# Gated cross-attention with a mixture of experts: TensorE's wait for its own last mix product is taken out

## The reference

```python
xn = layernorm(layernorm(x), gamma, beta)
q = (xn @ w_q).reshape(B, SQ, 16, 64)
k, v = split(context @ w_kv)
attn = softmax(einsum('bqhd,bkhd->bhqk', q * 64 ** -0.5, k))
out = einsum('bhqk,bkhd->bqhd', attn, v).reshape(B, SQ, 1024) @ w_out + b_out
x = x + tanh(g_xattn) * tanh(gate) * out
...
logits = layernorm(x) @ gate_w.T + gate_b
weights, selected = top_k(softmax(logits), 2)       # experts 8 and 9 are null
x = x + tanh(g_ffn) * sum over the chosen e of weight_e * (layernorm(x) @ expert_w[e] + expert_b[e])
```

## Time and profile before

| | |
|---|---|
| median of 3 runs | 1507.19 us (1505.58 to 1510.52) |
| span of the profiled execution, first to last instruction | 1490.5 us |
| TensorE busy | 1322.5 us, 7181 products |
| VectorE busy | 1148.4 us |
| ScalarE busy | 795.4 us |
| GpSimd busy | 707.9 us |

### The profile page before, as it was taken

The page is one execution under the profiler, slowest core; times in us unless marked ns, Lnnn a source line. Parts: engine busy times, 40 slices in busy tenths (PEclk is TensorE's granted clock), DMA queues, the critical chain, the costliest instruction groups (busy, mean ns, idle before and its releaser), DMA issues. The chain is left out here.

```text
span 1490.5 us, 31236 instructions
## 1 busy us (share of the span) xinstructions
PE 1322.5 (89%) x7181; PEld 677.1 (45%) x7182; DVE 1148.4 (77%) x2891; ACT 795.4 (53%) x2843; POOL 707.9 (47%) x651
## 2 busy tenths in 40 slices
PE   5576699999999999999999999998069998899997
PEld 3422254444444444444444444543035554455543
DVE  5877688889888888889889888986447775567765
ACT  5765566656555655665566556663244442344442
POOL 0360123244544444454454454354457774666675
PEclk9896899999999999999999999999579999999999
DMA  5895588799887788987787977766344443677773
GB/s 192 223 249 171 159 171 194 185 210 216 214 203 171 177 208 197 239 192 172 179 218 197 239 171 178 178 162 146 136 127 159 156 151 100 219 250 232 243 237 113
DMA packets 415499, 280.70 MB, mean 188 GB/s; under 512 B 319965, under 2 KB 348701, under 8 KB 415054
## 3 DMA queue, kind: packets, MB, share of 16 engines
q1 hardware_dynamic: 387598, 205.85, 56.3%
q0 software_dynamic: 27840, 74.18, 15.8%
HBM read 123.62 MB, written 83.07 MB: 139 GB/s over the span
## 5 line engine op out<-in xcount | busy, mean ns | idle before, releaser
L952 ACT ACTIVATE expd<-scores,less 128x77 f32<-128x77 f32 x1024 | 317.3, 328 | 229.9 <-DVE less L1048 228.8
L851 PE MATMUL scores<-m_sb,zT 128*128 (+2 forms) x2304 | 416.3, 339 | 21.8 <-PEq L156 9.6
L866 PE MATMUL mix<-u_sb,pT 128*128 128x512 f16 x1728 | 383.5, 380 | 0.5 <-DVE x_out L1073 0.4
L1792 PE MATMUL out_bank<-w_parts,m_sb 128*128 x1440 | 336.1, 384 | 1.2 <-issue 0.4
L851 PEld LDWEIGHTS scores<-m_sb,zT 128*128 128x128 f16 x2304 | 223.6, 98 | 190.9 <-issue 30.5
L866 PEld LDWEIGHTS mix<-u_sb,pT 128*128 128x128 f16 x1728 | 168.8, 98 | 197.8 <-DVE x_out L1073 0.7
L952 ACT ACTIVATION_READ_ACCUMULATOR expd<-scores,less 128x1 f32 x1024 | 213.4, 208 | 0.0
L1792 PEld LDWEIGHTS out_bank<-w_parts,m_sb 128*128 128x128 f16 x1440 | 142.2, 99 | 151.2 <-issue 12.0
L1485 POOL DMA_INDIRECT table<-payload,row_i x128 | 159.2, 1244 | 54.3 <-issue 33.5
L1399 POOL TENSOR_TENSOR z_parts<-z,z_parts 128x512 f16<-128x512 f32 x62 | 71.7, 1156 | 208.3 <-ACT z_parts L943 208.3
L1815 ACT CAST m_sb<-yT_bank 128x512 f16<-128x512 f32 x120 | 70.2, 585 | 173.3 <-PE yT_bank L1779 173.3
(11 more groups left out here) (171 smaller groups left out, 1756.5 us busy)
## 6 DMA issues: line engine op xcount, KB each, us to landing
comb<-x_out SPq DMA_DIRECT2D x64, 512.0 KB, 3.2
x_ln<-in_x_dram SPq DMA_DIRECT2D x64, 256.0 KB, 2.7
x_res<-in_x_dram SPq DMA_DIRECT2D x64, 256.0 KB
w_raw<-in_L_ffn_expert_w_dram SPq DMA_DIRECT2D x64, 128.0 KB, 2.3
m_dram<-m_stage SPq DMA_DIRECT2D x32, 231.0 KB, 5.4
u_dram<-m_sb SPq DMA_DIRECT2D x48, 154.0 KB
m_sb<-m_dram SPq DMA_DIRECT2D x12, 616.0 KB
u_sb<-u_dram SPq DMA_DIRECT2D x6, 1024.0 KB, 5.4
```

Of the source, the lines that this page charges most:

```text
L851: last = pe.matmul(scores[s][k][:, 0:n], zT[:, s, zp, t, :], m, start=(t == 0 and (zp, mp) == PRODUCTS[0]), stop=(t == DT - 1 and (zp, mp) ...
L866: last = pe.matmul(mix[:], pT[:, s, pp, k, :], u_sb[:, k, up, :], start=(k == 0 and (pp, up) == PRODUCTS[0]), stop=False)
L952: last = act.activation(expd[:, s, h * KEYS:(h + 1) * KEYS], scores[s][k][:, at:at + KEYS], ACT.Exp, bias=less[:, s, h:h + 1], scale=1.0 / ...
L1792: last = pe.matmul(c.out_bank[s][:], yT[:, s, yp, t, :], w_parts[:, bass.ds(e, 1), t, wp, :].rearrange("p a n -> p (a n)"), start=(t == 0 ...
```

## The change

TensorE's wait and the release behind it are taken out, with the semaphore `mix_ready`. The two that waited for `mix_ready` now wait for `u_read`: the residual of tile i for its count 3i + 3, the turning of p of tile i for 3(i - 1), which is the last mix product of tile i-2. The wait points at the same product as before, without the way over TensorE's sequencer.

```diff
@@ semaphores @@
-        mix_ready = sem("mix_ready")
@@ turn_p_hi(i, s), SyncE @@
                 if later(i, 2):
 
-                    sp.wait_ge(mix_ready, i - 1)
+                    sp.wait_ge(u_read, 3 * (i - 1))
                     sp.nop(nofuse=True)
                 sp.dma_start_transpose(out=pT[:, s, 0], in_=p_parts[:, 0]).then_inc(pT_hi_in[s], 16)
@@ mix_values(i, s), TensorE @@
                 last.then_inc(u_read, 1)
-                pe.wait_ge(u_read, 3 * i + 3)
-                pe.nop(nofuse=True).then_inc(mix_ready, 1)
@@ residual(i, s), VectorE @@
-                dve.wait_ge(mix_ready, i + 1)
+                dve.wait_ge(u_read, 3 * i + 3)
                 dve.wait_ge(x_res_in[s], 8 * (i - s) + 16)
```

## The result

| | before | after |
|---|---|---|
| median of 4 runs | 1508.86 us (1505.58 to 1511.04) | 1464.6 us (1459.26 to 1475.45) |
| ratio, 95% interval | | 0.9708 [0.9675, 0.9741] |
| time of the profiled execution, its span | not given, 1490.5 us | 1463.94 us, 1462.2 us |

The change saves 44.3 us, 2.9%. The forecast was 1470 us with a range of 1465 to 1485, so the time came out 0.4 us under the range. The sign and the place came as forecast, and so did what TensorE gains. The gain was 7 us larger than the sum, because the limit that VectorE was to set was reckoned too early.

A forecast was written before the change was run, and what follows sets the result against it. TensorE was taken to pace attention, losing 3.3 us per loop iteration, with the gain capped by VectorE: 38.6 - 1.5 = 37 us off the 1490.5 us span gives 1453.5, plus 16.7 around it, 1470 us; range 1465 to 1485.

The forecast's parts named there:

- the sum: Attention stage: VectorE's idle time on TensorE, 30.3 + 3.4 + 4.9 = 38.6 us, less 1.5 for small costs: 37 us gained.
- the limit that VectorE was to set: Attention loop: VectorE alone would need 51.8 us per iteration, above TensorE's 51.05, so the gain ends there.
- TensorE paces the stage before: Attention stage: TensorE is never held by anyone and sets the pace, with VectorE close behind.
- Two losses: TensorE between mix and gate: drain, 0.31 us a written-out step, plus register work; 3.3 us per loop iteration go in all.
- only the drain goes: Rival, 15%: between mix and scores, register work and jump stay visible behind the gate; gain 24.6 us, time 1482.5 us.
- 2.04 us before the residual and 0.23 before the scores' maximum: VectorE's idle time on TensorE per loop iteration; with 0.24 for overlap, 2.51 us off 54.35.
- VectorE is late next and takes over the pace: Attention loop after the change: VectorE's 51.8 us per iteration, above TensorE's 51.05, sets the pace; case given 72%.
- the room of some 5.6 us: Attention: with one mix bank TensorE may get some 5.6 us ahead, more than VectorE's steps are uneven.
- mix <- x_out: Sign on TensorE's wait list: this wait for VectorE's reading of the mix appears, with several us.
- The small terms: VectorE's extra register instructions 0.5 us, later u loads at the three batch changes 1 us; 1.5 us subtracted.
- The 16.7 us around the span: Outside the profiled span: 1507.2 - 1490.5 us, if the profiled execution was like the median, and it stays.
- the prediction's first rival: Drain alone goes, 15%, 1482.5 us; by the skill's 166 ns per product 64 x 0.166 = 10.6 us, 1496.6.

The follow-up runs named there:

- experiment 6: A 320-column VectorE multiply added per step: on the kernel before 1490.96 us, ratio 1.0004; on the kernel after 1461.23 us, ratio 0.9803.
- experiment 5: Kernel before plus a second TensorE wait for its own product, behind the first group of u's rows inside the mix: 1509.07 us, ratio 1.0114.
- Experiment 4: Kernel after plus a TensorE wait at the old place, for an older product, five before the mix's last: 1446.59 us, ratio 0.9713.
- experiment 3: Kernel after plus the wait for the last mix product, put behind the gate's eight products: 1479.86 us, ratio 0.9932 to before.
- Experiment 2: Kernel after with TensorE's wait for its last mix product put back, without the release; readers still wait for u_read: 1486.87 us, ratio 0.9985.
- Experiment 8: Kernel after without the mix's last product: 1443.46 us, ratio 0.9704; also with less_top's multiply by a number, one input: 1443.84 us, ratio 0.9700.
- experiment 1: Both kernels rerun unchanged on one chip: before 1488.78 us, ratio 0.9997; after 1447.45 us, ratio 0.9704.
- experiment 7: Kernel after with less_top's multiply by a number, one input: 1444.25 us, ratio 0.9703; also with an extra 320-column VectorE multiply per step: 1457.95 us, ratio 0.9799.

## Why the prediction was right and where it failed

**TensorE paces the stage before: right.** 0.32 us more per step on VectorE cost nothing there (experiment 6), 0.31 us more on TensorE cost 19 us (experiment 5).

**Two losses, the drain (the 0.31 us until TensorE's last product counts as written) and the register work behind it, and both go: right.** The gate begins 0.22 us and the scores 0.42 us after the last product, in the loop and at the jump as forecast. Experiment 4 shows that the same sequencer work is free with a wait that is met early, experiment 3 that it costs 0.28 us, and 0.77 with the jump, behind a wait that isn't. The estimate of 51.05 us for TensorE's iteration measured 51.08. The rival "only the drain goes" is refuted. The Trainium skill, "Advanced Engine Details and Errata", section "Engine Queue Depths", gives TensorE's queue 64 entries; by that the sequencer can be past gate and jump, and the full gain agrees with it.

**Only the readers' half could have done it: no.** Experiment 2 gave some 2 us.

**The step that failed** is "In one iteration it sat 0.95 + 0.45 + 0.64 = 2.04 us before the residual and 0.23 before the scores' maximum", the term from which VectorE's own 51.8 us an iteration and the sum of 38.6 came. It took the list of waits for the whole of VectorE's waiting, and the list leaves out short ones. Two rows of before that I had not set side by side, TensorE's first score bank and VectorE's first maximum:

```profile
618.01 2.51 PE L851 MATMUL scores<-m_sb,zT 128*128 x12 [0.23 <-issue]
```

```profile
634.15 0.64 DVE L1046 TENSOR_REDUCE top<-scores 128x6 f32<-128x462 f32 x1
```

A bank of 12 products takes 2.51 us; the scores of the step at 631.60 have theirs at 634.11, and the maximum begins at 634.15, 0.04 behind it: it waited, and has no bracket. The same 0.04 stands at 593.59 and 607.14 (banks at 593.55 and 607.10), and only the last of these has a bracket, 0.23.

From x_out to the first maximum the four steps took 3.30, 3.27, 3.07 and 3.17 us before, and take 3.14, 2.95, 2.95 and 2.95 after (575.91 - 572.77 and so on): 0.82 us less an iteration where I had 0.23 (the 0.12 of the third step has another cause, which stays open: no bank was awaited there). The rest of each step, from the first maximum to the next x_out, became 1.03, 0.03, 0.53 and 0.72 us shorter: the waits of 0.95, 0.45 and 0.64 with 0.08 each, as reckoned. So the one term that was mis-sized is the 0.23, which is 0.82, 0.70 of it in steps where the maximum waited for its bank.

With it VectorE's own iteration is 54.35 - 2.51 - 0.59 = 51.25 us, measured 51.21. Over the loop that is 12 x 0.59 = 7.1 us more than the 38.6 of the sum, 45.7. Experiment 8 bears it out: with 14 us less for TensorE to do the stage is 832.4 - 786.2 = 46.2 us shorter than before. This is more than the 44.2 us that TensorE has to give, so it is TensorE's loss and not VectorE's idle time that bounds the gain.

**"VectorE is late next and takes over the pace": wrong as a consequence.** With 51.21 against 51.08 us VectorE falls back by 0.13 us an iteration, 1.6 us over the loop, and the room of some 5.6 us that one mix bank leaves (an estimate of the prediction) holds that; TensorE waited for x_out for 0.9 us in all, at the stage's end. So the gain is TensorE's whole loss, 12 x 3.27 + 16 x 0.31 = 44.2 us. VectorE's 51.21 us aren't all work: they hold 1.05 + 1.30 + 0.22 + 0.35 = 2.9 us of waiting for ScalarE's exponentials, which start from VectorE's own maxima, so the two together are what comes next. The several us of "mix <- x_out" that I expected on TensorE didn't come for the same reason; and where VectorE does pace (experiment 8), TensorE waits at the ranks.

**The small terms.** Of the 0.5 us for register instructions and 1 us for the changes of batch nothing is seen; with them the sum was 1.5 us further off. u's big loads did land later, in 7.7 us (median of six) where it was 5.4, but no mix waited for them. The DMA share rose from 0.82 to 0.87 in the earlier trace rows's stretch, and no engine waited for a turning in the loop. The clock stayed at 1.00.

**The 16.7 us around the span: wrong, without effect.** They are 1.7. The other 15 were the profiled execution's distance from the median. Since the gain was subtracted from the median, the forecast didn't suffer.

**The other signs.** The first x_out that comes earlier is tile 6's, as forecast: tile 5's is at 265.90 before and 266.06 after, tile 6's at 278.94 and 278.24.

## What to carry to other kernels

An in-order engine should not wait for its own newest result only to pass the news on: the wait costs the drain, 0.31 us here, and brings the sequencer work behind it into view; together it was 0.81 us in one loop step and 1.04 where the loop jumps back. Let the readers wait for the product's own count, or wait for an older product (1.08 us older was free). To find where such a gain ends, measure the next engine's waits by setting its start against the end of what it reads, row by row; the wait list leaves out the short ones, and a few tenths of a microsecond in 54 decided here which engine bounds the gain.

## What the hardware showed beside this

VectorE's tiny operation `less` lasts 0.17 us, but 1.07 in one step of four. In the kernel after (experiment 1), first VectorE's rows and then GpSimd's of the same time:

```profile
590.79 0.76 DVE L1130 TENSOR_TENSOR gap<-largest 128x8 f32<-128x8 f32 x1
...
593.20 1.07 DVE L1045 TENSOR_TENSOR less<-top,minus_scale 128x5 f32<-128x5 f32 x1
```

```profile
590.37 1.15 POOL L1396 TENSOR_TENSOR z_parts<-z,z_parts 128x512 f16<-128x512 f32 x1 [2.89 <-ACT z_parts L940]
593.10 1.15 POOL L1405 TENSOR_TENSOR y_parts<-y,y_parts 128x512 f16<-128x512 f32 x1
```

`gap` ends at 591.55 and GpSimd's operation at 591.52; `less` at 594.27 and GpSimd's at 594.25. From 280 to 980 us, `less` on the two banks of five heads begins 14 times inside such an operation of GpSimd and then lasts 1.07 to 1.12 us, and 96 times outside and then lasts 0.16 or 0.17. This is also why experiment 6's operation cost 1.07 us in one step and nothing in the others: there it pushed `less` from just ahead of GpSimd's operation to just behind its start, and in the other steps a hold that ends at GpSimd's pace became shorter instead (in the third step `gap` lasts 0.53 us, not 0.76, and `less` 0.95, not 1.07). That GpSimd is the cause is argued from these times; no run moved its work away. The Trainium skill, "SBUF — State Buffer", section "SBUF: two separate sides", says that the two engines share a port pair as an exclusive lock, which the one that starts first keeps for its whole instruction; VectorE needs it for an operation in a two-port mode, or with two SBUF inputs while GpSimd's reads SBUF. For the form with two inputs the rows agree (1.07 us inside GpSimd's operation, 0.17 outside). The form with one input and five elements in fp32 was held as long (1.08 us, experiment 7); whether it ran in a two-port mode no run here shows, so one input alone doesn't free an operation from the hold.

Second, "TensorE: Matmul & The Clock Gate", section "Single matmul latency", of the Trainium skill puts a product's fixed part at 166 ns. The gap that a wait for the own last product leaves is 0.31 us here, in the written-out steps before and in experiment 5. The page's figure is for one product alone and not for such a wait; taken for its price, as in the prediction's first rival, it gave half of what was measured.
